# Attention on one core: the weighting of a quad two quads behind its scores, between the two halves of another quad's scores, and the diagonal blocks dealt to other column groups

## The chip, the cores and the metric

The kernel is one launch on one core of a Trainium2 chip. Its time is the device time of an execution in microseconds (us). A core has TensorE (PE, with its weight loads shown apart as PEld), VectorE (DVE), ScalarE (ACT), GpSimd (POOL), and SyncE (SP), which here only issues DMAs. The engines run their own instruction streams in order and wait for each other through semaphores.

## The reference, cut to what matters

One post-norm decoder layer on 2048 tokens of width 256: causal self-attention with 16 heads of depth 16, then a linear cross-attention against 1601 context rows, then a mixture of 8 experts (top 2) and a shared expert, each followed by a layer norm.

```python
scores = jnp.einsum('bhqd,bhkd->bhqk', q, k) / jnp.sqrt(jnp.float32(Dh))
scores = jnp.where(causal[None, None], scores, jnp.float32(-jnp.inf))
attn = jax.nn.softmax(scores, axis=-1)
out = jnp.einsum('bhqk,bhkd->bhqd', attn, v)
```

Only the attention stage is touched by the change. It is computed for 16 heads (`H`), 2048 queries and keys, lower triangle only.

## The kernel before, in words

`project` makes queries, keys and values and finds the row maxima of head 0, and some of head 1. `attend` computes the attention, `finish` everything behind it. The three are blocks: the next starts when the one before has ended on all engines.

In `attend` a head is cut into 10 quads (`QUADS`, line 51): a quad is a block of 512 queries against 512 keys, that is four key tiles of 128. The quads, numbered 0 to 9, are (0,0), (1,0), (1,4), (2,0), (2,4), (2,8), (3,0), (3,4), (3,8), (3,12), as query block and first key tile; quads 0, 2, 5 and 9 lie on the diagonal, and they are the last of their query block (`LAST_QUAD`). A score tile has the keys on its partitions and the queries along its row. The scores of a quad come in two halves of two tiles (`scores_half`, line 723), each half in its own PSUM buffer of two banks; the two tiles of a half run beside each other in the upper and the lower half of TensorE's rows, since a tile contracts over 49 rows only. On the diagonal, tile j has only 512 - 128 j queries, and two small matmuls (line 739) hide what is above the diagonal. ScalarE takes the exponential of each half (`exps`, line 683) into `probs`. TensorE then weights the values with them (`weigh`, line 744): four float32 matmuls, one for each key tile, each into 32 of the 128 partitions of the one bank `acc`, so that the four stand in four column groups of the array; each shows as two weight loads and two matmuls in the trace, eight in all for a weighting. Column group j sums the tiles j of all quads of a query block. When a query block is done, ScalarE copies `acc` away (`copy_acc`, line 695), and the first weighting of the next query block waits for that copy (`acc_copied`, line 749), since there is one `acc`.

Between these, the same TensorE works on the next heads' row maxima, which the softmax of a head needs before it starts. For these it forms the scores again with the queries on the partitions, in 35 pieces a head (`PIECES`), most of 512 columns, four of 384, each into one of three PSUM banks, the ring (`NRING = 3`, `through_ring`, line 775; the matmuls are at lines 151 and, for the diagonal blocks, 158). VectorE reduces each piece to its maximum (line 169), and entry e of the ring waits until entry e - 3 has been taken. The table `PLACES` (line 88) says which pieces stand where: each of the ten quads has three places, one behind the first half of its scores, one behind the second half, and one at its end. A letter w, d, n, p or q is a piece, M the turning of the maxima into a row, F the fold of a head's four column groups into one (line 762, through a ring bank too, taken by ScalarE, line 704), T the turning of the folded result (line 769). The pieces of quads 6 to 9 are those of the head after next, the others those of the next.

The order on TensorE for quad q is written out in the loop at the end of its block: first half of the scores, first place, second half, second place, the weighting of quad q - 1, third place. A half of the scores waits for the exponential of the same half of the quad before. `probs` has two buffers, by the parity of the quad, and the first exponential of a quad waits for the weighting of two quads before.

Of the kernel before, what the change touches and what calls it, by code (L numbers as in the profile page):

```python
# [8 lines left out]
H = 16  # L9
# [4 lines left out]
P = 128  # L14
DC = D // P
NT = S // P
QB = 512
NQ = S // QB
TPQ = QB // P
# [32 lines left out]
NQUAD = len(QUADS)  # L52
# [23 lines left out]
VW = 32  # L76
LAST_QUAD = [max(s for s, (b, _) in enumerate(QUADS) if b == qb) for qb in range(NQ)]
STACK_DMAS = 16 * 2 * 2 * SLOTS
NRING = 3
SCORE_TILES = ((0, 1), (2, 3))  # L80
DIAGONAL_TILES = ((0, 3), (1, 2))

# [495 lines left out]
def attend(nc, f32, f16, bf16, ALU, ACT, X, q_split, k_split, w_all, w_split_d, res, bo_rows, ident32, attn, values,  # L578
# [6 lines left out]
    with es:  # L585
        def sb(name, shape, dt):
            return es.enter_context(nc.sbuf_tensor(name, shape, dt))
# [1 line left out]
        def sem(name):  # L589
            return es.enter_context(nc.semaphore(name))  # L590

        probs = sb("probs", [P, 2, TPQ * QB], f32)
        acc_sb = sb("acc_sb", [P, 2, NQ, QB], f32)
        folded = sb("folded", [P, QB], f32)
        inv = sb("inv", [P, 2, TPQ, NQ, 1], f32)
# [22 lines left out]
        def halves_of(s):  # L618

            qb, k0 = QUADS[s]  # L620
            if k0 != qb * TPQ:
                return [[(j, j % 2 * QB, QB) for j in half] for half in SCORE_TILES]
            return [[(j, QB - (QB - P * j) if (j, n) == (1, 0) else n * QB, QB - P * j) for n, j in enumerate(half)]
                    for half in DIAGONAL_TILES]

        def span(s, half):

# [54 lines left out]
        @block.scalar  # L682
        def _(act):
            def exps(h, s):
                quad = h * NQUAD + s
                for half in range(2):
                    first, w = span(s, half)
                    act.wait_ge(scores_ready, 2 * (2 * quad + half + 1))
                    if half == 0 and quad >= 2:
                        act.wait_ge(pv_done, quad - 1)  # L690
                    at = half * 2 * QB + first
                    nc.scalar.activation(probs[:, s % 2, at:at + w], scores[half][:, first:first + w],  # L692
                                         ACT.Exp, scale=QK_SCALE).then_inc(exp_done, 1)

            def copy_acc(h, qb):
                act.wait_ge(pv_done, h * NQUAD + LAST_QUAD[qb] + 1)
                nc.scalar.activation(acc_sb[:, h % 2, qb], acc[:], ACT.Copy).then_inc(acc_copied, 1)  # L697

            def copy_folded(h):
                e = ENTRY_AT["fold", h, 0]  # L700
                act.wait_ge(ring_ready, e + 1)
                if h > 0:
                    act.wait_ge(ring_ready, ENTRY_AT["turn", h - 1, 0] + 1)
                nc.scalar.activation(folded[:], ring[e % NRING][:], ACT.Copy).then_inc(fold_copied, 1)

            for h in range(H):
                for s in range(NQUAD):
                    exps(h, s)
                    if s == 0 and h > 0:
                        copy_acc(h - 1, NQ - 1)  # L710
                    for qb in range(NQ - 1):
                        if s == LAST_QUAD[qb] + 1:
                            copy_acc(h, qb)
                    if h > 0 and s == FOLD_AT:
                        copy_folded(h - 1)
            copy_acc(H - 1, NQ - 1)
            copy_folded(H - 1)

        @block.tensor
        def _(pe):  # L720
            def scores_half(h, s, half):
                qb, k0 = QUADS[s]
                quad, slot = h * NQUAD + s, h % NSTACK
                if quad >= 1:
                    pe.wait_ge(exp_done, 2 * (quad - 1) + half + 1)
                diagonal = k0 == qb * TPQ
                for group, (j, at, w) in enumerate(halves_of(s)[half]):
                    kt = k0 + j
                    used = group_rows(group, MROW + 1)
                    mm = nc.tensor.matmul(scores[half][:, at:at + w], kstack[used, slot, kt * P:(kt + 1) * P],  # L730
                                          qstack[used, slot, (qb + 1) * QB - w:(qb + 1) * QB],
                                          start=True, stop=not diagonal)
                    if not diagonal:
                        mm.then_inc(scores_ready, 1)
                if diagonal:
                    for part, b in enumerate((GROUP, P)):
                        for group, (j, at, w) in enumerate(halves_of(s)[half]):
                            copy, used = hide_half(group, part), group_rows(group, GROUP)
                            mm = nc.tensor.matmul(scores[half][:, at:at + b], ident16[used, copy],  # L739
                                                  hide_queries[used, copy, 0:b], start=False, stop=part == 1)  # L740
                            if part == 1:
                                mm.then_inc(scores_ready, 1)

            def weigh(h, s):
                qb, k0 = QUADS[s]
                pe.wait_ge(exp_done, 2 * (h * NQUAD + s) + 2)
                first, last = k0 == 0, s == LAST_QUAD[qb]
                if first and h * NQ + qb > 0:
                    pe.wait_ge(acc_copied, h * NQ + qb)
                if qb == 0:  # L750
                    for j in range(1, TPQ):
                        nc.tensor.matmul(acc[VW * j:VW * (j + 1), 0:P * j], zeros16[:, 0:VW], ones16[:, 0:P * j],
                                         start=True, stop=True)
                for j, at, w in sorted((j, half * 2 * QB + at, w) for half in range(2) for j, at, w in halves_of(s)[half]):
                    mm = nc.tensor.matmul(acc[VW * j:VW * (j + 1), QB - w:QB], values[:, h, k0 + j],  # L755
                                          probs[:, s % 2, at:at + w], start=first, stop=last)
                mm.then_inc(pv_done, 1)

            def fold_sums(bank, h):
                pe.wait_ge(acc_copied, (h + 1) * NQ)  # L760
                for b in range(NQ):
                    mm = nc.tensor.matmul(bank[VW * b:VW * (b + 1), :], fold[:], acc_sb[:, h % 2, b],
                                          start=True, stop=True)
                return mm

            def turn_sums(bank, h):
                pe.wait_ge(fold_copied, h + 1)
                for t in range(TPQ):
                    mm = nc.tensor.transpose(bank[:, t * P:(t + 1) * P], folded[:, t * P:(t + 1) * P], ident32[:])
                return mm  # L770

            given = [0, 0]

            def through_ring(items):
                for item in items:
                    kind, g, n = item
                    e = ENTRY_AT[item]
                    bank = ring[e % NRING]
                    if e >= NRING:
                        wait_taken(pe, e - NRING)  # L780
                    if kind == "piece":
                        group = given.index(min(given))
                        given[group] += WIDTH[n]
                        mm = form_piece(nc, bank, qstack, kstack, ident16, hide_keys, g % NSTACK, n, group)
                    elif kind == "max":
                        pe.wait_ge(max_found, g)
                        mm = nc.tensor.transpose(bank[0:NT, 0:P], neg_max[:], ident32[:])
                    elif kind == "fold":
                        mm = fold_sums(bank, g)
                    else:  # L790
                        mm = turn_sums(bank, g)
                    mm.then_inc(ring_ready, 1)

            for h in range(H):
                pe.wait_ge(max_in, h * MAX_DMAS + MAX_DMAS)
                for s in range(NQUAD):
                    ahead = h + (2 if s in EARLY_QUADS else 1)
                    if ahead < H and s in (0, EARLY_QUADS[0]):
                        pe.wait_ge(stack_in[ahead % NSTACK], (ahead // NSTACK + 1) * STACK_DMAS)
                    for half in range(2):  # L800
                        scores_half(h, s, half)
                        given[:] = [w for _, _, w in halves_of(s)[half]]
                        through_ring(RING[h][s][half])
                    if h * NQUAD + s > 0:
                        weigh(*divmod(h * NQUAD + s - 1, NQUAD))
                    through_ring(RING[h][s][2])
            weigh(H - 1, NQUAD - 1)
            through_ring(RING_END)

        @block.vector  # L810
# [989 lines left out]
```

## Time and profile before

| | us |
|---|---|
| median of 3 runs (lowest to highest) | 844.12 (843.93 to 846.46) |
| the profiled execution, its own time | 844.39 |
| its span, first to last instruction | 842.7 |
| start of `attend`'s first scores in it | 88.9 |
| start of the stage behind `attend` | 474.8 |

The mean granted TensorE clock is 0.986 of full speed over the span. Times in the trace are counted from the span's start, so the profiled execution has 1.7 us outside the span. A head's stretch is taken here from its first scores to the first scores of the next head. In rows of the trace the columns are named in the group's line; "busy" of an engine is the union of its instructions' times, and matmuls overlap, their ends being modelled.

### The profile page before, as it was taken

To read this page: it belongs to the slowest core of one execution; us is meant where nothing else is said; L and a number is where in the kernel's file an instruction comes from. 1 tells how busy PE (TensorE), PEld (TensorE's weight loads), DVE (VectorE), ACT (ScalarE), POOL (GpSimd) and SP (SyncE) were. 2 spreads that over 40 slices of the span, in tenths; PEclk is the share of its full clock that TensorE was granted. 3 is DMA by queue.
4 is the path that set the end of the run, shared out by engine and by line. 5 is a ranking of instruction groups with operands and counts; after the bars stand their busy time and mean duration, and the time that the engine had idled before them with its cause. 6 is when DMAs were issued, how large, how long until landed. Compare 5 with 4: busy or idle time off the path is not lost. (4 is left out here: it accounts for less than half of the span.)

```text
span 842.7 us, 19213 instructions
## 1 busy us (share of the span) xinstructions
PE 791.3 (94%) x7242; PEld 480.7 (57%) x7243; DVE 556.1 (66%) x1072; ACT 512.9 (61%) x756; POOL 304.2 (36%) x226
## 2 busy tenths in 40 slices
PE   5899999999999999999998798989999999999994
PEld 2366333333333333333332486778888888877883
DVE  4575789999999999999980397973333333222395
ACT  4441687777887877778879587335444444453543
POOL 5050594555434355554541012132333333301121
PEclk9999999999999999999999999999999999999997
DMA  9783244234444433334332498373432222321372
GB/s 300 129 220 139 113 152 127 91 112 138 139 151 152 151 115 109 112 130 141 114 114 113 164 422 196 128 247 59 77 76 75 76 75 76 75 58 50 96 201 75
DMA packets 68360, 111.44 MB, mean 132 GB/s; under 512 B 39485, under 2 KB 49918, under 8 KB 63934
## 3 DMA queue, kind: packets, MB, share of 16 engines
q1 hardware_dynamic: 63134, 93.36, 36.5%
q0 software_dynamic: 4816, 16.65, 5.7%
q10 hardware_dynamic: 336, 0.40, 0.4%
q8 instruction: 52, 0.85, 0.4%
q14 instruction: 22, 0.18, 0.1%
HBM read 66.60 MB, written 32.37 MB: 117 GB/s over the span
## 5 line engine op out<-in xcount | busy, mean ns | idle before, releaser
L169 DVE TENSOR_REDUCE partial<-ring 128x1 f32<-128x512 f32 (+3 forms) x509 | 308.8, 669 | 30.0 <-PE ring L151 21.1
L692 ACT ACTIVATE probs<-scores 128x1024 f32<-128x1024 f32 (+1 forms) x320 | 270.9, 904 | 63.1 <-PE scores L739 32.6
L755 PE MATMUL acc<-probs,values 128*32 128x512 f32 (+3 forms) x1280 | 170.1, 541 | 0.9 <-ACT acc_sb L697 0.7
L1263 ACT ACTIVATE hid<-turned 128x512 f32<-128x512 f32 (+1 forms) x112 | 65.5, 584 | 161.3 <-PE turned L1424 127.7
L1664 DVE TENSOR_TENSOR work<-hid,work 128x512 f16<-128x512 f32 (+1 forms) x112 | 76.8, 690 | 124.9 <-ACT work L1268 100.3
L1449 PE MATMUL ops<-weights,work 128*128 (+1 forms) x1320 | 149.1, 273 | 2.7 <-issue 2.1
L151 PE MATMUL ring<-kstack,qstack 48*128 48x512 f16 (+1 forms) x580 | 143.8, 350 | 2.1
L1424 PE MATMUL turned<-mats,weights 128*128 128x256 f16 (+1 forms) x1344 | 144.0, 262 | 1.9 <-DMA mats<-attn 1.1
L1449 PEld LDWEIGHTS ops<-weights,work 128*128 128x128 f16 x1320 | 128.2, 98 | 19.3 <-issue 3.9
L667 POOL TENSOR_TENSOR a_w_in<-a_w_in,w_scale 128x2304 f32<-128x2304 f32 x16 | 64.4, 4027 | 206.4 <-DMA a_w_in<-w_all 206.4
L1424 PEld LDWEIGHTS turned<-mats,weights 128*128 (+1 forms) x1344 | 122.3, 98 | 20.5 <-issue 3.5
L730 PE MATMUL scores<-qstack,kstack 49*128 49x512 f16 (+3 forms) x640 | 126.6, 350 | 3.9 <-ACT probs L692 2.6
L151 PEld LDWEIGHTS ring<-kstack,qstack 48*128 48x128 f16 x580 | 44.2, 94 | 91.6 <-DVE partial L169 81.8
L1188 POOL DMA_INDIRECT by_token<-attn,dest_u x39 | 38.7, 991 | 143.3 <-DVE attn L1673 137.5
L730 PEld LDWEIGHTS scores<-qstack,kstack 49*128 49x128 f16 x640 | 39.8, 93 | 80.4 <-ACT probs L692 62.2
L672 POOL TENSOR_TENSOR a_w_out<-a_w_in,a_w_out 128x2304 f16<-128x2304 f32 x16 | 73.1, 4568 | 1.3
L1268 ACT ACTIVATE work<-hid 128x512 f16<-128x512 f32 (+1 forms) x112 | 69.7, 623 | 4.7
L158 PE MATMUL ring<-hide_keys,ident 64*128 64x128 bf16 x460 | 51.2, 202 | 0.0
L158 PEld LDWEIGHTS ring<-hide_keys,ident 64*128 64x128 bf16 x460 | 41.2, 95 | 16.8 <-issue 0.2
L1180 POOL DMA_INDIRECT attn<-rows_d,token_u x39 | 38.5, 987 | 29.0 <-issue 11.0
L739 PE MATMUL scores<-hide_queries,ident 64*128 64x64 bf16 (+1 forms) x512 | 44.0, 204 | 0.0
L697 ACT ACTIVATE acc_sb<-acc 128x512 f32<-128x512 f32 x64 | 38.7, 605 | 8.3 <-PE acc L755 8.3
(203 smaller groups left out, 702.2 us busy)
## 6 DMA issues: line engine op xcount, KB each, us to landing
a_w_in<-w_all SPq DMA_DIRECT2D x16, 1152.0 KB, 8.0
w_split_d<-a_w_out SPq DMA_DIRECT2D x16, 1152.0 KB, 5.7
weights<-w_split_d SPq DMA_DIRECT2D x6, 2048.0 KB, 19.7
weights<-w_split_d POOLq DMA_DIRECT2D x3, 2048.0 KB
qstack<-q_split SPq DMA_DIRECT2D x72, 64.0 KB, 2.6
kstack<-k_split SPq DMA_DIRECT2D x72, 64.0 KB, 2.8
weights<-by_token SPq DMA_DIRECT2D x8, 512.0 KB, 8.3
attn<-xT SPq DMA_DIRECT2D x4, 512.0 KB, 7.5
```

Source lines behind the costliest of these rows:

```text
L151: mm = nc.tensor.matmul(bank[:, at:at + w], qstack[rows, slot, t * P:(t + 1) * P], kstack[rows, slot, c:c + w], start=True, stop=not diagonal)
L158: mm = nc.tensor.matmul(bank[:, at - P + a:at - P + b], ident16[rows, copy], hide_keys[rows, copy, a:b], start=False, stop=part == 1)
L169: return nc.vector.tensor_reduce(out=found[:, places[0]:places[-1] + 1:step], in_=bank[:, 0:WIDTH[n]].rearrange("p (k w) -> p k w", k=len( ...
L672: nc.gpsimd.tensor_tensor(w_out[:, h % 2, 1], w_in[:, h % 2], w_out[:, h % 2, 0], ALU.subtract).then_inc(w_lo, 1)
L692: nc.scalar.activation(probs[:, s % 2, at:at + w], scores[half][:, first:first + w], ACT.Exp, scale=QK_SCALE).then_inc(exp_done, 1)
L730: mm = nc.tensor.matmul(scores[half][:, at:at + w], kstack[used, slot, kt * P:(kt + 1) * P], qstack[used, slot, (qb + 1) * QB - w:(qb + 1) ...
L755: mm = nc.tensor.matmul(acc[VW * j:VW * (j + 1), QB - w:QB], values[:, h, k0 + j], probs[:, s % 2, at:at + w], start=first, stop=last)
L1263: nc.scalar.activation(h32, hps[b].rearrange("p (j n) -> p j n", n=TW)[:, :, 0:w], ACT.Silu, scale=1.0 / WSCALE).then_inc(silu_done, 1)
L1268: nc.scalar.activation(hid[:, parity, 0, b * HB:(b + 1) * HB, 0:w], h32, ACT.Copy).then_inc(hid_hi, 1)
L1424: mm = nc.tensor.matmul(place.rearrange("p (g n) -> p g n", n=P), weights[:, a, bass.ds(at + (k * HID + (b * HB + j) * P), P)], turned_row ...
L1449: mm = nc.tensor.matmul(bank[:, i], hid[:, parity, a, j, i * P:(i + 1) * P], weights[:, c, bass.ds(at + (WE // 2 + j * D), D)], start=(m = ...
L1664: nc.vector.tensor_tensor(hid[:, parity, 1, chunks, 0:w], hid32[:, b % 2].rearrange("p (j n) -> p j n", n=TW)[:, :, 0:w], hid[:, parity, 0 ...
```

## The change

In words: the weighting of a quad comes one quad later than before, and within the quad it stands between the first place and the second half of the scores, not behind the second place. `probs` has three buffers, and the copies of `acc` on ScalarE stand one quad later as well. The last two weightings of the last head come behind everything. In a weighting of a diagonal quad of query blocks 1 to 3, key tiles 0 and 1 (512 and 384 queries) keep only their last 320 queries in their own column group; the first 192 of tile 0 go to column group 3, the first 64 of tile 1 to column group 2. `PLACES` is the same as before, and so is the ring.

```diff
+LAG = 2
+NPROBS = LAG + 1
...
-        probs = sb("probs", [P, 2, TPQ * QB], f32)
+        probs = sb("probs", [P, NPROBS, TPQ * QB], f32)
...
+        def weighings(s):
...
+            qb, k0 = QUADS[s]
+            own, given_away = [], []
+            for j, at, w in sorted((j, half * 2 * QB + at, w) for half in range(2) for j, at, w in halves_of(s)[half]):
+                more = w - (QB + P) // 2 if k0 == qb * TPQ and qb > 0 else 0
+                if more > 0:
+                    given_away.insert(0, (TPQ - 1 - j, j, at, QB - w, more))
+                    at, w = at + more, w - more
+                own.append((j, j, at, QB - w, w))
+            return own + given_away
...
-                    if half == 0 and quad >= 2:
-                        act.wait_ge(pv_done, quad - 1)
+                    if half == 0 and quad >= NPROBS:
+                        act.wait_ge(pv_done, quad - NPROBS + 1)
...
-                    if s == 0 and h > 0:
+                    if s == LAG - 1 and h > 0:
                         copy_acc(h - 1, NQ - 1)
                     for qb in range(NQ - 1):
-                        if s == LAST_QUAD[qb] + 1:
+                        if s == LAST_QUAD[qb] + LAG:
                             copy_acc(h, qb)
...
-                for j, at, w in sorted((j, half * 2 * QB + at, w) for half in range(2) for j, at, w in halves_of(s)[half]):
-                    mm = nc.tensor.matmul(acc[VW * j:VW * (j + 1), QB - w:QB], values[:, h, k0 + j],
-                                          probs[:, s % 2, at:at + w], start=first, stop=last)
+                parts = weighings(s)
+                for n, (group, j, at, first_query, w) in enumerate(parts):
+                    mm = nc.tensor.matmul(acc[VW * group:VW * (group + 1), first_query:first_query + w], values[:, h, k0 + j],
+                                          probs[:, quad % NPROBS, at:at + w], start=first,
+                                          stop=last and group not in [x[0] for x in parts[n + 1:]])
...
                         through_ring(RING[h][s][half])
-                    if h * NQUAD + s > 0:
-                        weigh(*divmod(h * NQUAD + s - 1, NQUAD))
+                        if half == 0 and h * NQUAD + s >= LAG:
+                            weigh(*divmod(h * NQUAD + s - LAG, NQUAD))
                     through_ring(RING[h][s][2])
-            weigh(H - 1, NQUAD - 1)
+            for s in range(NQUAD - LAG, NQUAD):
+                weigh(H - 1, s)
```

## Rows read from the trace of the kernel before

**Rows 1.** Busy time by engine, in five stretches (columns named in the first line).

```profile
core 0: us, PE busy (x) PEld busy (x) DVE busy (x) ACT busy (x) POOL busy (x), PEclk, DMA share, GB/s
209.56:233.70 24.14, 23.99 (x245) 9.13 (x244) 22.20 (x40) 19.14 (x25) 10.97 (x4) 1.00 0.42 133
257.84:281.98 24.14, 23.99 (x246) 9.11 (x243) 22.20 (x40) 19.14 (x25) 11.85 (x4) 1.00 0.40 133
426.76:448.83 22.07, 21.30 (x207) 7.18 (x204) 14.05 (x26) 18.76 (x25) 10.70 (x3) 1.00 0.26 90
448.83:474.78 25.95, 21.11 (x191) 6.50 (x187) 1.37 (x4) 20.19 (x28) 0.01 (x1) 1.00 0.20 81
```

**Rows 2.** VectorE in that head, in order: start, length, idle before and releaser.

```profile
212.54 4.15 DVE L169 TENSOR_REDUCE partial<-ring 128x1 f32<-128x512 f32 x7 [0.29 <-PE ring L151]
216.99 3.68 DVE L169 TENSOR_REDUCE partial<-ring 128x1 f32<-128x512 f32 x6 [0.30 <-PE ring L158]
221.58 2.35 DVE L169 TENSOR_REDUCE partial<-ring 128x1 f32<-128x512 f32 x4 [0.90 <-PE ring L151]
224.38 5.04 DVE L169 TENSOR_REDUCE partial<-ring 128x1 f32<-128x512 f32 x8 [0.20 <-PE ring L151]
229.57 0.26 DVE L815 RECIPROCAL inv<-ring 128x16 f32<-128x16 f32 x1
229.87 0.42 DVE L817 TENSOR_TENSOR attn<-ring,inv 128x256 f32<-128x256 f32 x1
```

**Rows 3.** Weight loads in order, 210 to 218.4: start, length, idle before.

```profile
210.52 0.09 PEld L151 LDWEIGHTS ring<-kstack,qstack 48*128 48x128 f16 x1 [0.19 <-DVE partial L169]
...
210.92 0.16 PEld L755 LDWEIGHTS acc<-probs,values 128*32 128x32 f32 x8
211.90 0.10 PEld L730 LDWEIGHTS scores<-qstack,kstack 49*128 49x128 f16 x2 [0.82 <-ACT probs L692]
...
212.13 0.10 PEld L730 LDWEIGHTS scores<-qstack,kstack 49*128 49x128 f16 x2
...
212.87 0.10 PEld L752 LDWEIGHTS acc<-ones,zeros 128*32 128x32 bf16 x3 [0.43 <-issue]
212.88 0.28 PEld L755 LDWEIGHTS acc<-probs,values 128*32 128x32 f32 x8
213.86 0.09 PEld L151 LDWEIGHTS ring<-kstack,qstack 48*128 48x128 f16 x1 [0.69 <-DVE partial L169]
```

**Rows 4.** TensorE's matmuls in order around two weightings and behind a fold.

```profile
216.27 0.39 PE L730 MATMUL scores<-qstack,kstack 49*128 49x512 f16 x2
...
217.02 0.38 PE L151 MATMUL ring<-kstack,qstack 48*128 48x512 f16 x1
...
217.32 1.04 PE L755 MATMUL acc<-probs,values 128*32 128x512 f32 x8
...
221.15 0.39 PE L151 MATMUL ring<-kstack,qstack 48*128 48x512 f16 x2
```

**Rows 5.** Groups in one head, 209.56 to 233.70: count, busy us, mean ns, idle before.

```profile
L692 ACT ACTIVATE probs<-scores 128x1024 f32<-128x1024 f32 x12 | 11.7, 1032 | 2.0 <-PE scores L730 2.0
L755 PE MATMUL acc<-probs,values 128*32 128x512 f32 x56 | 10.6, 604 | 0.0
L755 PE MATMUL acc<-probs,values 128*32 128x384 f32 x8 | 3.3, 495 | 0.0
L697 ACT ACTIVATE acc_sb<-acc 128x512 f32<-128x512 f32 x4 | 2.4, 605 | 0.5 <-PE acc L755 0.5
```

**Rows 6.** ScalarE in order, 216 to 219.5.

```profile
216.72 1.94 ACT L692 ACTIVATE probs<-scores 128x1024 f32<-128x1024 f32 x2 [0.56 <-PE scores L730]
218.55 0.60 ACT L697 ACTIVATE acc_sb<-acc 128x512 f32<-128x512 f32 x1
```

More of the change, by code:

```diff
@@ L688, in exps @@
                     act.wait_ge(scores_ready, 2 * (2 * quad + half + 1))
-                    if half == 0 and quad >= 2:
-                        act.wait_ge(pv_done, quad - 1)
+                    if half == 0 and quad >= NPROBS:
+                        act.wait_ge(pv_done, quad - NPROBS + 1)
                     at = half * 2 * QB + first
-                    nc.scalar.activation(probs[:, s % 2, at:at + w], scores[half][:, first:first + w],
+                    nc.scalar.activation(probs[:, quad % NPROBS, at:at + w], scores[half][:, first:first + w],
                                          ACT.Exp, scale=QK_SCALE).then_inc(exp_done, 1)
@@ L745, in weigh @@
                 qb, k0 = QUADS[s]
-                pe.wait_ge(exp_done, 2 * (h * NQUAD + s) + 2)
+                quad = h * NQUAD + s
+                pe.wait_ge(exp_done, 2 * quad + 2)
                 first, last = k0 == 0, s == LAST_QUAD[qb]
```

## The prediction

> **What bounds the kernel now.** I first cut the span by stage. The attention stage takes 385.9 us (88.9 to 474.8), and a head in it 24.14 us, the same from head to head [rows 1]. In such a head TensorE is busy 23.99 us and VectorE 22.20, ScalarE only 19.14. The busy share makes TensorE look like the bound, and a reader would expect lighter matmuls to be paid back in full. The order of VectorE's instructions says otherwise. It reduces piece after piece with eight short holes, the largest 0.29, 0.30, 0.90 and 0.20 us [rows 2], and the 1.94 us that are no busy time (24.14 - 22.20) are all that a head could lose while VectorE's work stays as it is. TensorE for its part stands still for VectorE: the piece at 210.52 follows idle time that a reduce ended [rows 3]. So the two are coupled by a ring of only three banks, and a head lasts as long as VectorE's 22.20 us plus the holes. Each hole stands behind a weighting, when the three banks have run dry before TensorE forms the next piece. I therefore price the change by those holes.
>
> **The durations.** The reduces of full pieces follow each other every 0.60 us: six take 3.68, the last one 0.68 of it [rows 2]. A weighting holds TensorE 0.98 us from its first load to the next instruction's (210.92 to 211.90, 212.88 to 213.86 with the zeroing in it) [rows 3]. From a last piece to the weighting it is 0.30 us (217.02 to 217.32), from a piece to its reduce 0.43 (221.15 to 221.58) [rows 2, 4]. A half of scores takes 0.22 to 0.23 (211.90 to 212.13) [rows 3]. On the diagonal, counting its columns at the same rate, 0.29 for the first half and 0.24 for the second.
>
> **What the change removes.** In a diagonal weighting of query blocks 1 to 3 the longest column group falls from 512 to 320 queries. The rows put a weighting at 1.04 us for four groups beside each other although the matmuls of the 512-wide tiles alone last 2 x 0.60 [rows 4, 5]: the groups run together and the longest sets the time. A full weighting streams about 0.85 us of its 0.98 (0.98 less some 0.1 to change over), so 192/512 of it is 0.32 us, three times a head, 0.96 us a head. The two added matmuls per weighting lie inside that. The saving is bounded by 0, if only the sum over the groups counted, and 0.32; I take 0.32, since the groups overlap in the trace. The Trainium skill, "TensorEngine Tiling (Array Packing)", Key Properties, says that tiles operate independently; by it the saving is the full 0.32, and the trace's overlap agrees. The number of changes between row halves and column groups stays two per quad, so nothing is gained or lost there.
>
> The later place takes away the waits of a weighting for its exponentials. They cost next to nothing today: ScalarE is idle 5 us a head [rows 1], and the weightings' matmuls show no idle time ahead of them in this head [rows 5]. The third buffer frees ScalarE from a wait that it doesn't have either. The scores' own waits for exponentials (a few of 0.1 us) stay or shrink. All together 0 to 0.3 us a head; I take 0.1. DMAs, SyncE's and GpSimd's work are not moved.
>
> **What it adds, first: every weighting is now followed by scores.** Today, behind the weighting of quad q - 1 comes the third place; in quads 1, 3, 4, 7, 8 and 9 that is a ring entry at once, and in all but the fold's case the hole is at most 0.1. After the change the weighting is followed by the second half of the scores in all ten quads, and preceded, where the first place is empty (quads 0, 2, 4, 5, 9), by the first half too. At best, the last piece in front of the weighting started the moment its bank came free. Then VectorE has just begun one reduce and has two more, 3 x 0.60 less 0.13 = 1.67 us from the piece's start. The next reduce starts at 0.30 + 0.98 + 0.22 + 0.43 = 1.93. That is a hole of 0.26. With a half of scores between piece and weighting it is 0.48, with a diagonal one 0.55. A lightened weighting takes 0.32 off.
>
> I lay the head out with these durations, place by place, each piece held until entry e - 3 is reduced. The holes, named by the weighting they stand behind, come to: quad 8's (quad 9's two-diagonal piece and a diagonal half ahead of it) 0.72; 9's, lightened, 0; 0's 1.23 (below); 1's 0.25; 2's 0.31, as too few pieces were waiting; around the fold, which now has pieces close on both sides, 0.12 in place of today's 0.90; 3's 1.14, for the fold took a bank and 1 us, and only one reduce is left when this weighting starts; 4's 0.11; 5's, lightened, 0; 6's 0.90, since only the 0.68 us of normalising stand ahead of it [rows 2] with the turnings; 7's 0.54. The sum is 5.3 us. The same laying out of the present order gives holes of 2.06 us against the 1.94 read and puts the three largest where the trace has them (0.32, 0.33, 1.07), so I trust it to a few tenths of a microsecond a head.
>
> **Second: the copy of `acc` is now late.** The copy of a finished query block stands on ScalarE behind the second exponential of quad q + 2, whose scores come behind the weighting it copies. From these scores' start it is 0.45 us to the exponential (216.27 to 216.72), 0.92 until the next instruction on ScalarE (1.94 - 1.02), 0.60 for the copy [rows 4, 6], 0.04 to release: 2.0 us until the next weighting may start. Queued behind that on TensorE is everything, the ring too. Today the copy starts as soon as the weighting ends and has a whole segment of pieces. For quad 0's weighting TensorE has only three pieces and a half of scores to do meanwhile, about 1.3 us with their waits for banks, so it stalls 0.7 us; this makes the 1.23 hole above. Behind quads 0, 2 and 5 there is enough to do (1.8 to 2.0). The cost is 0 to 1.1 us for one weighting, and I take 0.7, already in the 5.3.
>
> **The sum.** Per head 5.3 - 2.06 = +3.25 us in the holes; the 0.32s and the 0.1 are in it, since a hole is measured with them. Heads 0 to 13 have all places filled: 14 x 3.25 = 45.5. Head 14 has pieces only in quads 0 to 5; for it the layout gives +1.4. Head 15 has none, VectorE is out of it (1.37 us busy) [rows 1], and there 0.96 is saved, but three late copies now have nothing to hide behind (0.7 to 1.1 us each): between -1 and +3, I take +1. Head 0 starts with an empty ring: -1. Together +47: 844.4 + 47 = 891.4 us against the profiled execution's own 844.39, which is 0.3 over the median of the runs; I say 891.
>
> The Trainium skill, same page, PSUM Bottleneck, warns that a faster TensorE leaves the emptying of PSUM as the limit. By it the lighter weighting brings nothing by itself; this is the trace's reading too, 22.20 of 24.14 us.
>
> **The rivals.** *TensorE's work sets the time* (faster). For it: 23.99 of 24.14 us busy. Then the change gives 0.96 us in each of 15 heads, and the segments between weightings pair somewhat better over the row halves (the busier half's columns, counted from the code, are 22,592 instead of 23,488 a head, 9.4 instead of 9.8 us at 0.21 us for 512), 0.4 more: -14 to -20, so 824 to 830. Against it: VectorE's reserve of 1.94 us would have to be used up by three quarters, by an order that has a score half behind each weighting. The fold's 0.8 us is really gained, so part of it is real: 7%.
> *Gains and holes cancel* (same): if TensorE could run pieces past the held scores, or the queue were fuller than I think, each hole would be near the 0.26 or less, 2.6 in all, and a head at 24.1 to 24.5: 844 to 850, 6%.
> *Only the late copy counts* (slower, small): 0.7 to 1.1 us in each of 16 heads less the lighter weightings' share, 850 to 866. It decides if the holes of full banks stay at 0.1 as today: 10%.
> *The holes as laid out*, slower by 25 to 62: 77%. Among these a miss of 1 us a head moves 14 us.
>
> **The numbers.** 891 is the likeliest. From the first three cases 23% lie below 866; within the likeliest the low end is the hole of full banks everywhere (about 3.1, plus the copy's 0.7: +1.8 a head, 25 us) and the high one that of queues shorter than laid out (+4.2 a head, 60 us). The range 862 to 905 leaves out the faster and same cases and a little above. What a measurement can tell from no change is 0.3%, 2.5 us. Faster 0.08, same 0.04, slower 0.88.
>
> **What would show it.** Right: a head of 27 to 27.5 us; VectorE still 22.2 busy in it but five idle, with holes behind most weightings, the largest behind quads 0, 3 and 6; a wait of quad 0's weighting (the zeroing before it) for the copy of `acc`; lightened weightings at some 0.66 from first load to next instruction; the hole behind the fold gone. Wrong: a head under 24 with VectorE's idle under 1.5, or lightened weightings of 0.98, or holes at the same eight places as today.

## Result and profile after

The changed kernel takes 898.98 us (894.58 to 899.79, 4 runs) against 844.02 (842.98 to 846.46, 4 runs): the ratio is 1.064, 95% interval 1.0617 to 1.0662. It is slower by 55 us; 891 was forecast, with 862 to 905 as the range.

The span grew by 54.4 us (842.7 to 897.1), and `attend` holds nearly all of it: 439.8 us (88.82 to 528.64) instead of 385.8 (88.95 to 474.78). The later stage moved by 0.5. First comes the busy time of the changed kernel by head (heads 0, 5, 14 and 15), with the same columns as [rows 1]. The changed kernel's lines are numbered otherwise: L172 is the reduce (L169 before), L154 and L161 a piece (L151, L158), L747 the scores (L730), L709 the exponentials (L692), L714 the copy of `acc` (L697), L770 and L774 the zeroing and the weighting (L752, L755).

```profile
88.82:117.38 28.56, 25.21 (x218) 9.63 (x220) 20.20 (x35) 19.56 (x24) 23.14 (x7) 0.82 0.23 86
227.35:254.84 27.49, 24.48 (x256) 10.03 (x254) 22.40 (x40) 19.37 (x25) 10.69 (x3) 1.00 0.36 116
474.78:498.78 24.00, 21.22 (x218) 8.19 (x216) 14.38 (x26) 18.64 (x25) 10.70 (x3) 1.00 0.25 90
498.78:528.64 29.86, 23.34 (x211) 8.06 (x211) 1.37 (x4) 20.84 (x28) 0.00 (x0) 0.89 0.15 61
```

A full head lasts 27.49 us instead of 24.13. The second number is TensorE: 24.48 of 27.49, where [rows 1] has 23.99 of 24.14, so it now stands idle as well. VectorE has as much to do as before (22.40 against 22.20; the 39 instructions are as long as before in sum, but fewer of the reduces overlap end to start) and is idle 5.1 us. Next, VectorE in head 5 of the changed kernel, the answer to [rows 2]:

```profile
229.56 4.14 DVE L172 TENSOR_REDUCE partial<-ring 128x1 f32<-128x512 f32 x7 [0.69 <-PE ring L154]
235.04 2.48 DVE L172 TENSOR_REDUCE partial<-ring 128x1 f32<-128x512 f32 x4 [1.33 <-PE ring L154]
237.88 1.29 DVE L172 TENSOR_REDUCE partial<-ring 128x1 f32<-128x512 f32 x2 [0.36 <-PE ring L154]
239.42 2.64 DVE L172 TENSOR_REDUCE partial<-ring 128x1 f32<-128x512 f32 x4 [0.25 <-PE ring L154]
243.03 1.16 DVE L172 TENSOR_REDUCE partial<-ring 128x1 f32<-128x512 f32 x2 [0.97 <-PE ring L154]
...
244.47 4.89 DVE L172 TENSOR_REDUCE partial<-ring 128x1 f32<-128x512 f32 x8
...
251.05 2.35 DVE L172 TENSOR_REDUCE partial<-ring 128x1 f32<-128x512 f32 x4 [0.82 <-PE ring L154]
253.88 1.29 DVE L172 TENSOR_REDUCE partial<-ring 128x1 f32<-128x512 f32 x2 [0.49 <-PE ring L154]
```

The holes stand behind the weightings of quads 8, 0, 1, 2, 3, 6 and 7, in this order; behind those of quads 4, 5 and 9 no single one is over 0.06 us (three behind quad 4's make 0.13 together). Every one was ended by a piece of TensorE's, that is, the ring had run dry. Then TensorE's weight loads around two weightings of this head, a lightened one and quad 0's, which answer to [rows 3]:

```profile
230.62 0.58 PEld L774 LDWEIGHTS acc<-probs,values 128*32 128x32 f32 x12 [0.23 <-issue]
231.31 0.10 PEld L747 LDWEIGHTS scores<-qstack,kstack 49*128 49x128 f16 x2
...
232.10 0.09 PEld L154 LDWEIGHTS ring<-kstack,qstack 48*128 48x128 f16 x1 [0.29 <-DVE partial L172]
...
233.39 0.13 PEld L770 LDWEIGHTS acc<-ones,zeros 128*32 128x32 bf16 x3 [0.91 <-ACT probs L709]
233.43 0.28 PEld L774 LDWEIGHTS acc<-probs,values 128*32 128x32 f32 x8
234.41 0.10 PEld L747 LDWEIGHTS scores<-qstack,kstack 49*128 49x128 f16 x2 [0.69 <-ACT probs L709]
```

The lightened weighting (twelve loads now) holds TensorE for 0.69 us (230.62 to 231.31) instead of 0.98. Quad 0's comes after a standstill: the zeroing's loads follow 0.91 us without one. What it waited for shows in the matmuls and on ScalarE, whose rows stand next:

```profile
233.42 0.34 PE L770 MATMUL acc<-ones,zeros 128*32 128x128 bf16 x3 [0.79 <-ACT acc_sb L714]
```

```profile
231.77 1.02 ACT L709 ACTIVATE probs<-scores 128x1024 f32<-128x1024 f32 x1 [0.72 <-PE scores L747]
232.69 0.59 ACT L714 ACTIVATE acc_sb<-acc 128x512 f32<-128x512 f32 x1
```

Scores of quad 1's second half start at 231.31, their exponential at 231.77, the copy of `acc` at 232.69; it ends at 233.28, and the zeroing's loads follow at 233.39. That is 2.1 us from the scores to the weighting, with TensorE idle for 0.79 of them.

### The profile page after: what moved, and what is told of

The parts are those of the page before. It is cut to its first block and busy times, and to the rows that moved or that the text cites. A ratio compares the mean times of both kernels' runs of the same rounds, so it can differ in the third digit from the quotient of the medians.

```text
span 897.1 us, 19596 instructions
## 1 busy us (share of the span) xinstructions
PE 803.4 (90%) x7434; PEld 497.9 (56%) x7435; DVE 559.0 (62%) x1072; ACT 518.2 (58%) x756; POOL 303.8 (34%) x226
## 5 line engine op out<-in xcount | busy, mean ns | idle before, releaser
L172 DVE TENSOR_REDUCE partial<-ring 128x1 f32<-128x512 f32 (+3 forms) x509 | 310.5, 668 | 77.7 <-PE ring L154 76.0
L709 ACT ACTIVATE probs<-scores 128x1024 f32<-128x1024 f32 (+1 forms) x320 | 276.6, 898 | 125.0 <-PE scores L756 70.3
L154 PE MATMUL ring<-kstack,qstack 48*128 48x512 f16 (+1 forms) x580 | 144.0, 351 | 28.9 <-DVE partial L172 26.4
L774 PE MATMUL acc<-probs,values 128*32 128x512 f32 (+2 forms) x1472 | 158.6, 501 | 3.3 <-ACT acc_sb L714 2.3
L747 PE MATMUL scores<-qstack,kstack 49*128 49x512 f16 (+3 forms) x640 | 132.0, 357 | 4.5 <-ACT probs L709 2.8
L747 PEld LDWEIGHTS scores<-qstack,kstack 49*128 49x128 f16 x640 | 38.5, 94 | 111.7 <-ACT probs L709 100.3
L154 PEld LDWEIGHTS ring<-kstack,qstack 48*128 48x128 f16 x580 | 46.6, 94 | 80.9 <-DVE partial L172 72.6
L774 PEld LDWEIGHTS acc<-probs,values 128*32 128x32 f32 x1472 | 44.3, 109 | 39.0 <-issue 27.0
L1694 DVE COPY attn<-ops 128x512 f32<-128x512 f32 (+1 forms) x20 | 13.6, 678 | 68.8 <-PE ops L1470 68.8
L161 PE MATMUL ring<-hide_keys,ident 64*128 64x128 bf16 x460 | 50.0, 203 | 0.0
L161 PEld LDWEIGHTS ring<-hide_keys,ident 64*128 64x128 bf16 x460 | 39.9, 95 | 16.7 <-issue 0.7
```

The source lines that it names most:

```text
L154: mm = nc.tensor.matmul(bank[:, at:at + w], qstack[rows, slot, t * P:(t + 1) * P], kstack[rows, slot, c:c + w], start=True, stop=not diagonal)
L161: mm = nc.tensor.matmul(bank[:, at - P + a:at - P + b], ident16[rows, copy], hide_keys[rows, copy, a:b], start=False, stop=part == 1)
L172: return nc.vector.tensor_reduce(out=found[:, places[0]:places[-1] + 1:step], in_=bank[:, 0:WIDTH[n]].rearrange("p (k w) -> p k w", k=len( ...
L709: nc.scalar.activation(probs[:, quad % NPROBS, at:at + w], scores[half][:, first:first + w], ACT.Exp, scale=QK_SCALE).then_inc(exp_done, 1)
L774: mm = nc.tensor.matmul(acc[VW * group:VW * (group + 1), first_query:first_query + w], values[:, h, k0 + j], probs[:, quad % NPROBS, at:at ...
```

## Experiments

Twelve further kernels, each timed beside the kernel before, and their ratio to it.

| kernel | us (lowest to highest) | ratio, 95% interval | full head, us |
|---|---|---|---|
| spread_only | 841.09 (840.89 to 842.11) | 0.9956 (0.9938 to 0.9973) | 23.86 |
| old_place | 840.98 (839.28 to 844.62) | 0.9965 (0.9947 to 0.9983) | 23.87 |
| no_spread | 907.25 (906.28 to 908.26) | 1.0735 (1.0712 to 1.0757) | 28.17 |
| early_copy | 879.73 (878.83 to 880.43) | 1.0407 (1.0386 to 1.0428) | 26.50 |
| after_table | 852.14 (850.79 to 853.60) | 1.0097 (1.0073 to 1.0120) | 24.19 |
| early_table | 838.45 (836.96 to 839.25) | 0.9923 (0.9903 to 0.9943) | 23.67 |
| light_before | 824.66 (824.05 to 831.53) | 0.9765 (0.9743 to 0.9787) | 22.91 |
| light_after | 859.94 (859.21 to 860.80) | 1.0184 (1.0161 to 1.0207) | 24.95 |
| light_early | 827.46 (826.48 to 828.81) | 0.9791 (0.9766 to 0.9816) | 22.90 |
| old_table | 831.20 (829.38 to 831.62) | 0.9836 (0.9816 to 0.9856) | 23.07 |
| spread_table | 834.03 (832.20 to 835.78) | 0.9869 (0.9845 to 0.9893) | 23.17 |
| table_only | 838.65 (838.34 to 841.79) | 0.9941 (0.9927 to 0.9954) | 23.65 |

The kernels with `light` in the name leave out part of the reduces; those with `table` have another `PLACES`. A full head is one of heads 1 to 13 in the profiled execution.

**Is it the place, the lag or the spreading?** spread_only has the spreading alone:

```diff
-LAG = 2
+LAG = 1
...
-                        if half == 0 and h * NQUAD + s >= LAG:
-                            weigh(*divmod(h * NQUAD + s - LAG, NQUAD))
+                    if h * NQUAD + s >= LAG:
+                        weigh(*divmod(h * NQUAD + s - LAG, NQUAD))
```

> The kernel before with one part of the change: the diagonal weightings spread over the column groups; lag 1, two probs buffers and the old place (behind the second place of the quad) stay. Theory (VectorE and the ring's holes set a head, 22.2 us busy plus holes): most of the 0.96 us a head saved on TensorE is waiting for the ring, a head goes from 24.13 to about 23.8, in all 840 us (835 to 844). Rival (TensorE's work sets a head): 0.96 us in each of 15 to 16 heads, 829 to 830 us. If the column groups do not overlap, 844.

old_place is the same without the first two lines (`LAG` stays 2).

> The changed kernel with the weighting put back behind the second place of the quad (scores, place, scores, place, weighting, third place), but still two quads late, with three probs buffers, spread diagonals and copies of acc one quad later. Theory (what costs is that scores follow each weighting and that the copy waits for scores behind its weighting): everything is regained, within 4 us of spread_only, 838 to 845 us. Rival (the lag of two quads itself or the third buffer costs): stays above 870.

no_spread takes the spreading out of the changed kernel:

```diff
-                more = w - (QB + P) // 2 if k0 == qb * TPQ and qb > 0 else 0
+                more = w - (QB + P) // 2 if False else 0
```

> The changed kernel without the spreading: a diagonal weighting takes 0.98 us again, all else as changed. Theory: 0.32 us more in the holes that they stand before, those behind quads 2, 5 and 9, some of it taken by waiting for banks: 0.4 to 0.7 us a head, 906 to 910 us. Rival (TensorE sets it): 0.96 a head, 914. If the spreading saves nothing: 899.

All three came as the theory had them. With this table of places the place costs 58 us (898.98 against 840.98), the late copy of `acc` that it brings along included; the lag and the third buffer cost nothing (841.09 with lag 1, 840.98 with lag 2). The spreading gives 3.6 us by itself (0.27 us a head of 0.96), and 8 in the changed kernel (0.68 a head). Here is how spread_only's VectorE takes it (its head 208.35 to 232.21):

```profile
220.10 2.35 DVE L172 TENSOR_REDUCE partial<-ring 128x1 f32<-128x512 f32 x4 [0.90 <-PE ring L154]
```

The fold's hole is 0.90 us as in [rows 2]: TensorE arrives earlier at the weightings, but the ring has no free bank, and the holes that have another cause stay. The rival by which TensorE's work alone sets the time asked for 829.

**How much is the late copy?** early_copy changes ScalarE's order alone:

```diff
                     nc.scalar.activation(probs[:, quad % NPROBS, at:at + w], scores[half][:, first:first + w],
                                          ACT.Exp, scale=QK_SCALE).then_inc(exp_done, 1)
+                    if half == 0 and s == LAG - 1 and h > 0:
+                        copy_acc(h - 1, NQ - 1)
+                    for qb in range(NQ - 1):
+                        if half == 0 and s == LAST_QUAD[qb] + LAG:
+                            copy_acc(h, qb)
...
                     exps(h, s)
-                    if s == LAG - 1 and h > 0:
-                        copy_acc(h - 1, NQ - 1)
-                    for qb in range(NQ - 1):
-                        if s == LAST_QUAD[qb] + LAG:
-                            copy_acc(h, qb)
```

> The changed kernel with the copy of acc moved on ScalarE from behind both exponentials of its quad to between them, so that it no longer waits for the scores behind the weighting that it copies. Theory: the hole behind quad 0's weighting falls from 1.33 us to 0.6, the last head gains 2 us: about 0.7 a head, 885 to 890 us. Rival (the late copy is hidden by waits for banks anyway): 897 to 899. If the late copy is the main cost of the change: under 865.

It gave more than expected: 19.3 us, 879.73 instead of 885 to 890. VectorE's order in the same head of early_copy shows where:

```profile
225.10 4.15 DVE L172 TENSOR_REDUCE partial<-ring 128x1 f32<-128x512 f32 x7 [0.69 <-PE ring L154]
229.72 2.48 DVE L172 TENSOR_REDUCE partial<-ring 128x1 f32<-128x512 f32 x4 [0.47 <-PE ring L154]
232.43 1.29 DVE L172 TENSOR_REDUCE partial<-ring 128x1 f32<-128x512 f32 x2 [0.22 <-PE ring L154]
233.97 2.64 DVE L172 TENSOR_REDUCE partial<-ring 128x1 f32<-128x512 f32 x4 [0.25 <-PE ring L154]
237.57 1.16 DVE L172 TENSOR_REDUCE partial<-ring 128x1 f32<-128x512 f32 x2 [0.97 <-PE ring L154]
...
245.59 2.35 DVE L172 TENSOR_REDUCE partial<-ring 128x1 f32<-128x512 f32 x4 [0.81 <-PE ring L154]
248.43 1.29 DVE L172 TENSOR_REDUCE partial<-ring 128x1 f32<-128x512 f32 x2 [0.48 <-PE ring L154]
```

Compared with the changed kernel's rows above, the hole behind quad 0's weighting falls from 1.33 to 0.47 and the one behind quad 1's from 0.36 to 0.22; all others stay within 0.01 us. That is 1.00 us a head. The last head falls from 29.86 to 25.96 us; in it the changed kernel has some 7 us at half clock that early_copy has not (last section), so part of these 3.9 us is the clock's. So the early copy takes back 19 us of the 55, and 36 stay, as holes that are the same with either copy.

**Are those other holes the order of the ring?** after_table deals the same pieces to other places, with everything else as changed:

```diff
-PLACES = (("", "wd", ""), ("ww", "w", "nw"), ("", "ww", ""), ("dw", "w", "w"), ("", "ww", "Fwp"),
-          ("", "wn", ""), ("ww", "d", ""), ("ww", "n", "w"), ("qMT", "wd", "nw"), ("", "ww", "wp"))
+PLACES = (("", "w", ""), ("wn", "n", "ww"), ("pw", "ww", "w"), ("w", "wdd", ""), ("", "ww", "F"),
+          ("ww", "", ""), ("nww", "w", "p"), ("w", "nqM", "T"), ("ww", "w", "w"), ("d", "", "wdw"))
```

> The changed kernel with another table of places (PLACES) and nothing else: the same 35 pieces, fold and turns per head, dealt so that a piece or two stand behind the second half of nearly every quad's scores, the fold at the end of quad 4 behind them, the turning of the maxima and of the result parted. Theory (the change is slow because its order of the ring does not fit the new place of the weighting, so VectorE runs dry): most of the loss is regained with the weighting where the change put it; laid out with the same durations a head takes 23.5 us instead of 26.9, so 842 to 856 us. Rival (scores behind each weighting cost whatever the pieces' order): above 880.

It takes 852.14 us, as expected, with a head of 24.19 us where 23.5 were laid out: the table alone, at the new place and with the late copy still there, regains 47 of the 55 us. That is more than the 36 that early_copy left, so the two causes don't add up: this table also hides a good part of the late copy. One busy row of its head 5 beside the changed kernel's above:

```profile
210.99:235.18 24.19, 23.41 (x255) 10.48 (x253) 22.19 (x40) 19.30 (x26) 10.91 (x4) 1.00 0.42 132
```

VectorE's idle time is 2.0 us instead of 5.1. early_table has both remedies, the early copy and a table for it (("", "w", ""), ("wp", "w", "w"), ("w", "", "w"), ("ww", "", "wn"), ("w", "wdF", "nd"), ("ww", "w", ""), ("dn", "nww", ""), ("w", "", "wM"), ("Tww", "", "wqd"), ("w", "wp", "w")).

> The weighting where the change put it, diagonals spread, the copy of acc between the exponentials, and a table of places dealt for this order. Theory (both faults of the change are mended, nothing else is wrong with the place): a head of 23.2 to 23.7 us, 830 to 840 us, faster than the kernel before. Rival (the place behind the first half is bad in itself): above 844.

838.45 us is under the kernel before, so the place as such does not make the kernel slow. That it costs nothing is not shown: the best tables found for the old place, further below, give 831.20 and 834.03 us, also with spread diagonals, and whether a better table exists for the new place was not tried.

**What if VectorE is taken out?** In light_before and light_after the reduce of line 169 takes only the first 32 columns of each part of a piece:

```diff
-... .rearrange("p (k w) -> p k w", k=len(places)), axis=X, op=ALU.max)
+... .rearrange("p (k w) -> p k w", k=len(places))[:, :, 0:32], axis=X, op=ALU.max)
```

> The kernel before, with each reduce of a piece over only the first 32 columns of each of its parts instead of all (the row maxima are then not those of whole rows). It takes VectorE's time out of the ring. Theory: TensorE is close behind VectorE, so a head falls from 24.1 to about 22.6 us, 818 to 828 us. If TensorE alone set the time of the kernel before: 844.

> The changed kernel with the same short reduces (over 32 columns of each part only). Theory: the holes of VectorE no longer count, what stays is the late copies of acc (2.0 us from the scores to the next weighting, four times a head, with less beside them than before), so a head takes 24 to 25 us against light_before's 22.6: 845 to 860 us. If the ring's holes on VectorE were all of the slowdown: equal to light_before or up to 15 us under it. If they were none of it: 899.

light_early is light_after with early_copy's edit.

> light_after (the changed kernel, short reduces over 32 columns of each part) with the copy of acc between the two exponentials. With VectorE out of the way light_after still lost 2.0 us a head to light_before (24.95 against 22.91) and 4.2 in the last head. Theory: that rest is the late copies, so a head falls to 22.9 to 23.5 us, 823 to 834 us. Rival (it is TensorE's own order, less well paired row halves, or the exponentials): above 850.

The busy rows of a head of each, light_before, light_after and light_early in this order:

```profile
203.67:226.57 22.90, 22.90 (x245) 8.71 (x242) 6.97 (x39) 19.14 (x25) 10.77 (x4) 1.00 0.42 140
```

```profile
211.36:236.31 24.95, 22.90 (x256) 9.77 (x255) 6.63 (x39) 19.26 (x26) 10.89 (x4) 1.00 0.40 128
```

```profile
203.72:226.62 22.90, 22.69 (x256) 9.77 (x254) 6.63 (x39) 19.09 (x26) 11.09 (x4) 1.00 0.43 140
```

With VectorE at 7 us a head the kernel before has a head of 22.91, with TensorE busy to the last tenth. So the 24.13 are VectorE's and TensorE's together, and 1.2 us of them go with VectorE's load. The change costs 35 us there instead of 55 (859.94 against 824.66), and the early copy takes 32 of these 35 away, the clock's part in the last head again included (light_after has a stretch at half clock there, light_early none). light_after came in at the upper edge of what was expected for it, and light_before's head is 22.91 where 22.6 were expected. Without VectorE's load, then, 2.8 us are left beside the late copy. This sum has the spreading's gain in it. If a TensorE that is never idle gained the whole 3 x 0.29 us a head from it (an estimate from the loads above, some 14 us in 16 heads), the place itself would cost up to 17 us even here; no run separates the two. Of the 36 us that early_copy left, then, about half at least need VectorE's load.

**Filling the holes.** old_table is old_place with the table ("", "w", "w"), ("", "ww", "p"), ("wd", "w", "w"), ("", "ww", "nw"), ("n", "", "wdFw"), ("", "ww", ""), ("nw", "d", "w"), ("d", "n", "w"), ("qMTw", "w", "w"), ("", "ww", "wpw"):

> The weighting two quads behind, in the old place, diagonals spread (old_place), with another table of places: pieces spread more evenly over the places, the fold with a piece ahead of and behind it, so that few holes are left on VectorE. Theory (a head lasts as long as VectorE's 22.2 us plus the holes, 1.7 us of holes in old_place): a head of 22.6 to 23.1 us instead of 23.87, 822 to 832 us. Rival (TensorE's own work is the floor now, so filling VectorE's holes does nothing): 838 to 841.

spread_table is spread_only with ("w", "", "n"), ("", "wpw", "w"), ("", "ww", "w"), ("n", "w", "wd"), ("d", "w", "ww"), ("F", "ww", ""), ("wpw", "", "d"), ("", "ww", "wq"), ("MT", "wn", "nd"), ("", "ww", "ww"), and table_only has this table in the kernel before.

> The kernel before (weighting one quad behind, in the old place, two probs buffers) with spread diagonals and a table dealt for it, the fold at the start of quad 5. Theory (the lag of two quads brings nothing; the holes are what counts): the same as old_table (831.2) within 5 us, 826 to 836. Rival (the second quad of lag frees TensorE of waits for exponentials that the denser ring now shows): 838 or more.

> spread_table without the spreading: the kernel before with nothing changed but the table of places. Theory: with VectorE's holes filled (0.97 us a head in spread_table) TensorE's time counts more than in the kernel before, so leaving out the 0.96 us a head costs 0.4 to 0.7 us a head instead of 0.27: 838 to 844 us. If VectorE alone sets a head now: 834 like spread_table. If TensorE alone: 848 or more.

old_table is the fastest, 831.20 us, 1.6% under the kernel before. Its VectorE in a head, with 0.6 us of holes left (23.07 less 22.46 busy):

```profile
206.22 13.82 DVE L172 TENSOR_REDUCE partial<-ring 128x1 f32<-128x512 f32 x22
...
220.55 4.84 DVE L172 TENSOR_REDUCE partial<-ring 128x1 f32<-128x384 f32 x8 [0.25 <-PE ring L161]
```

Twenty-two reduces run through the fold without a hole that the view marks. table_only against spread_table prices the spreading once the holes are filled: 23.65 against 23.17 us a head, 0.48 instead of 0.27; in the times 4.6 us, with intervals that lie apart. old_table is 2.8 us under spread_table, with intervals that overlap; whether that is the lag, the other table or neither was not separated. spread_table and early_table have the same spreading, each with a table dealt for its place: 834.03 against 838.45 us, with intervals that lie apart.

## Why the prediction was right

**The bound.** Right in the main. That a head is VectorE's busy time plus its holes is true by definition; what the runs show is that the holes respond. 0.96 us a head less work for TensorE gave 0.27 (spread_only), another table alone gave 0.48 (table_only, 23.65 against 24.13), and VectorE's load taken away gave 1.22 (light_before). The last also shows that the reader of the busy shares is not far off: TensorE stands only 1.2 us behind. Two readings in the prediction are a little off. The head has nine holes over 0.02 us and not eight, and they don't all stand behind a weighting: the largest, 0.90, is behind the fold, and two of 0.03 are between VectorE's small instructions. Nor does the lighter weighting bring nothing by itself; it brings 3.6 us.

**The lightened weighting.** 0.98 to 0.69 us in the trace, 0.66 forecast, so 0.87 us a head rather than 0.96. The column groups do overlap. Of the 0.96 us a head, the ring took back 0.69 in spread_only. The rival of TensorE's work (824 to 830) fell with it.

**The scores behind each weighting.** The holes as laid out and as read in the changed kernel: behind quad 8's weighting 0.72 and 0.69, 9's 0 and 0, 0's 1.23 and 1.33, 1's 0.25 and 0.36, 2's 0.31 and 0.25, at the fold 0.12 and 0.03, 3's 1.14 and 0.97, 4's 0.11 and 0.13, 5's 0 and 0, 6's 0.90 and 0.82, 7's 0.54 and 0.49. The sum is 5.3 against 5.1 us. The three largest are behind the quads that the prediction named. A head grew by 3.36 us where 3.25 were forecast; in part this nearness is luck, since the holes grew by 3.15 (1.94 to 5.09) and VectorE's busy time, which the forecast held fixed, by 0.20. What the prediction did not see is that most of this is a misfit of table and place and not the place alone: it held `PLACES` fixed, as the change does, and after_table shows 3.3 us a head that hang on it.

**The late copy.** The mechanism was right, the size low. In a full head it is 1.0 us and not 0.7: 0.86 in the hole behind quad 0's weighting and 0.14 in the next. The rival that only the copy counts (850 to 866) is refuted: with the early copy the kernel still takes 879.73. So is the one by which gains and holes cancel (844 to 850).

**The sum.** Heads 1 to 13 gave 43.7 us (forecast 42.3). Head 0 gave 4.5 instead of 2.3, head 14 gave 1.9 instead of 1.4, and head 15 gave 3.9 instead of 1. These three make up 5.6 of the 7 us between 47 and 54. Head 15 is the term that was mis-sized most: early_copy brings it back to 25.96 us against 25.95 [rows 1], so its 3.9 is what the late copies lead to, where I had allowed 1 for them net of the spreading. The 0.96 that the spreading was to save there is too high as well: in spread_only this head is 25.61 us, 0.34 less than before. Part of the 3.9 is the clock: no_spread, with late copies and full clock in this head, has 28.68 us, 2.7 more than before.

## What to carry to other kernels

When two engines are coupled by a short ring, write down the consumer's idle stretches one by one and ask of a reordering which of them it opens. TensorE's busy share (99% here) did not say what lighter matmuls would bring: they brought 0.27 us a head of 0.96. A table that deals work to places belongs to the order it was dealt for: here moving the weighting past a place cost 58 us, and dealing the same pieces again gave 47 back. And look at what a copy that frees an accumulator is queued behind: here, moved ahead of an exponential whose scores come after the accumulation it copies, it gave 19 us.

## What was not expected of the hardware

The clock of TensorE fell for longer than before. These are stretches of the changed kernel, two of head 0 and one of head 15:

```profile
92.00:96.00 4.00, 3.89 (x29) 1.69 (x31) 2.31 (x5) 1.82 (x3) 2.04 (x1) 0.50 0.96 406
96.00:100.00 4.00, 4.00 (x21) 0.84 (x18) 2.48 (x4) 2.11 (x3) 3.94 (x2) 0.50 0.02 4
...
505.00:512.00 7.00, 6.02 (x38) 1.60 (x38) 0.00 (x0) 4.55 (x6) 0.00 (x0) 0.51 0.00 0
```

And the same two of head 0 in the kernel before:

```profile
92.00:96.00 4.00, 4.00 (x34) 1.72 (x37) 2.77 (x6) 2.60 (x5) 2.04 (x1) 0.59 1.00 424
96.00:100.00 4.00, 4.00 (x36) 1.05 (x32) 3.67 (x7) 3.42 (x5) 3.94 (x2) 1.00 0.02 4
```

Both kernels start head 0 with some microseconds at half clock, the 1.2 of the two levels 1.2 and 2.4 GHz; the kernel before is back at full clock at 96, the changed one is not at 100, and does 21 matmuls from 96 to 100 where the kernel before does 36. Its mean over head 0 is 0.82 against 0.93. In head 15, where the kernel before has 1.00 throughout [rows 1], the changed kernel runs seven microseconds at half clock behind its first waits for late copies, with TensorE busy 4.64 of the 6.22 us ahead of them:

```profile
498.78:505.00 6.22, 4.64 (x56) 2.05 (x58) 0.00 (x0) 4.89 (x7) 0.00 (x0) 1.00 0.71 288
```

no_spread has the late copies too, no such stretch, and a head 15 of 28.68 us, 1.2 less than the changed kernel's in spite of its longer weightings. light_after, with late copies and spreading, has one at the same point of its head 15, which lasts 30.14 us:

```profile
464.90:471.70 6.80, 5.82 (x36) 1.54 (x32) 0.00 (x0) 3.59 (x5) 0.00 (x0) 0.50 0.00 0
```

What the clock costs can be bounded from the four runs of the changed kernel. Three had a mean granted clock of 0.973 to 0.977 over the span and took 898.82 to 899.79 us; the fourth had 0.986, as the kernel before, and took 894.58. So some 4 to 5 of the 55 us go with the clock, and at the same clock the forecast of 891 is 3.6 us low and not 8. In which head the fourth run was faster is not known, since it has no trace; why the clock fell is not shown.
